# Three more filler products, and the weights' low part split before the second pair of inputs, in the opening of a GRU, attention and FFN kernel

## What is computed

```python
def cell(h, x):
    gi = x @ W_ih + b_ih
    gh = h @ W_hh + b_hh
    i_r, i_z, i_n = jnp.split(gi, 3, axis=-1)
    h_r, h_z, h_n = jnp.split(gh, 3, axis=-1)
    r = jax.nn.sigmoid(i_r + h_r)
    z = jax.nn.sigmoid(i_z + h_z)
    n = jnp.tanh(i_n + r * h_n)
    h_new = (1.0 - z) * n + z * h
    return (h_new, h_new)
```

## Time and profile before

| what | us |
|---|---|
| median of three runs | 617.98 |
| lowest and highest | 616.83, 618.19 |
| the profiled execution's own time | 617.67 |
| its span | 615.9 |

### The profile page before, as it was taken

The page is one execution under the profiler, slowest core; times in us unless marked ns, Lnnn a source line. Parts: engine busy times, 40 slices in busy tenths (PEclk is TensorE's granted clock), DMA queues, the critical chain, the costliest instruction groups (busy, mean ns, idle before and its releaser), DMA issues.

```text
span 615.9 us, 14207 instructions
## 1 busy us (share of the span) xinstructions
PE 581.6 (94%) x4918; PEld 526.5 (85%) x4918; DVE 516.6 (84%) x1544; ACT 404.8 (66%) x982; POOL 256.2 (42%) x401
## 2 busy tenths in 40 slices
PE   8999999999999879998888999999999999999997
PEld 7999999999999878887776888888888887888875
DVE  2776777776767768888988999999999999999996
ACT  3545454544445456575446888888888888888885
POOL 0333323232332353420144555555565565565550
PEclk9999999999999999998999999999999999999999
DMA  8400000000000000500000000000000000000001
GB/s 267 169 2 1 2 1 2 1 1 2 1 1 1 19 1 1 186 1 1 2 0 2 10 11 18 19 10 18 19 18 11 19 18 10 19 20 10 18 19 34
DMA packets 12517, 14.87 MB, mean 24 GB/s; under 512 B 1632, under 2 KB 10144, under 8 KB 12448
## 3 DMA queue, kind: packets, MB, share of 16 engines
q1 hardware_dynamic: 12448, 13.97, 6.8%
HBM read 9.78 MB, written 4.19 MB: 23 GB/s over the span
## 4 chain that ended last, share of the span: by engine, by line
PE 69%; DVE 13%; ACT 12%; issue 3%; SPq 1%; DMA 1%; POOL 0%; DVEq 0%; ACTq 0%
PE PS L451 22%; PE PS L313 16%; PE PS L336 12%; ACT q_s L756 4%; PE PS L503 3%; PE PS L524 3%; ACT k_s L737 2%; PE PS L487 2%; PE PS L429 2%; PE PS L389 2%; PE PS L372 2%; ACT big L669 2%; DVE PS L1052 1%; DVE big L934 1%; ACT PS L740 1%
## 5 line engine op out<-in xcount | busy, mean ns | idle before, releaser
L451 PE MATMUL PS<-k_s,h_s 128*128 128x128 f32 x1024 | 160.7, 285 | 4.6 <-DVE PS L1032 1.9
L451 PEld LDWEIGHTS PS<-k_s,h_s 128*128 128x128 f32 x1024 | 131.7, 191 | 22.0 <-DVE PS L1040 10.0
L313 PE MATMUL PS<-part 128*128 128x256 f32 x900 | 115.6, 286 | 0.0
L313 PEld LDWEIGHTS PS<-part 128*128 128x128 f32 x900 | 109.8, 191 | 0.0
L737 ACT ACTIVATE k_s<-h_s 128x128 f32<-128x128 f32 x256 | 69.1, 306 | 50.5 <-DVE h_s L1137 29.1
L336 PE MATMUL PS<-big,wrk 128*128 128x128 f32 x744 | 88.4, 275 | 2.2 <-DVE big L891 2.2
L336 PEld LDWEIGHTS PS<-big,wrk 128*128 128x128 f32 x744 | 85.8, 192 | 2.8 <-DVE big L891 2.8
L1200 POOL COPY h_s<-big 128x256 f32<-128x256 f32 x32 | 21.5, 671 | 131.2 <-DVE big L891 131.2
L451 PE MATMUL PS<-h_s 128*128 128x128 f32 x384 | 74.2, 275 | 0.0
L451 PEld LDWEIGHTS PS<-h_s 128*128 128x128 f32 x384 | 58.3, 192 | 0.0
L634 ACT ACTIVATE big<-big 128x256 f32<-128x256 f32 x32 | 13.3, 417 | 63.8 <-DVE big L873 63.8
(11 more groups left out here) (184 smaller groups left out, 1277.8 us busy)
## 6 DMA issues: line engine op xcount, KB each, us to landing
out<-q_s SPq DMA_DIRECT2D x32, 128.0 KB, 1.7
x_s<-in_xT SPq DMA_DIRECT2D x14, 256.0 KB, 6.1
k_s<-in_wgT SPq DMA_DIRECT2D x1, 832.0 KB, 5.2
k_s<-in_wuT SPq DMA_DIRECT2D x1, 832.0 KB, 7.1
k_s<-in_wih SPq DMA_DIRECT2D x3, 256.0 KB, 4.0
wrk<-in_whh SPq DMA_DIRECT2D x3, 256.0 KB, 4.9
h_s<-in_wdT SPq DMA_DIRECT2D x1, 768.0 KB, 7.6
x_s<-in_xT SPq DMA_DIRECT2D x4, 128.0 KB, 3.7
```

Source lines behind the costliest of these rows:

```text
L313: r = pe.matmul(p, y, x, start=i == 0, stop=i == len(passes) - 1)
L451: return pe.matmul(PS[:, m, 0:128], w, x, start=False, stop=True, skip_group_check=True)
```

## The change

Three edits, all in what is issued before the loop over the steps. SyncE issues the load of the last third of `W_hh` (gate z) behind the second pair of x, not ahead of it. TensorE makes eleven products of ones in place of eight. VectorE makes `wih_lo` right after `wih_hi`, ahead of the two splits of x. No instruction is removed, the computed result is the same, and every line of the kernel behind L256 has a number that is one higher.

```diff
-            for i in (0, 2, 1):
+            for i in (0, 2):
                 sp.dma_start(wcut(whh_s, i), wcut(kp(whh), i)).then_inc(ld_whh[i], 16)
             for k in range(2):
                 sp.dma_start(x0[:, k, 2:4], xv[:, k, 2:4, :]).then_inc(ld_x0[1], 16)
+            sp.dma_start(wcut(whh_s, 1), wcut(kp(whh), 1)).then_inc(ld_whh[1], 16)
...
-            keep_warm(0, 8)
+            keep_warm(0, 11)
...
             ve.tensor_copy(raw(wih_hi), wih_s).then_inc(s_wih, 1)
+            ve.wait_ge(s_wih, 1)
+            ve.tensor_tensor(raw(wih_lo), wih_s, wih_hi, ALU.subtract).then_inc(s_wih, 1)
             ve.wait_ge(ld_x0[1], 32)
             ve.tensor_copy(raw(x_hi[1]), x_s[:, :, 256:512]).then_inc(s_x1, 1)
             ve.wait_ge(s_x1, 1)
             ve.tensor_tensor(raw(x_lo[1]), x_s[:, :, 256:512], x_hi[1], ALU.subtract).then_inc(s_x1, 1)
-            ve.wait_ge(s_wih, 1)
-            ve.tensor_tensor(raw(wih_lo), wih_s, wih_hi, ALU.subtract).then_inc(s_wih, 1)
```

## The result

| what | changed | before |
|---|---|---|
| median of four runs, us | 614.06 | 617.40 |
| lowest and highest | 613.36, 614.19 | 616.18, 618.19 |
| the profiled execution's own time | 613.96 | 617.67 |
| its span | 612.0 | 615.9 |

The ratio is 0.9945, with a 95% interval of 0.9925 to 0.9966. Both have to be explained.

A forecast was written before the change was run, and what follows sets the result against it. The opening was taken as bound by VectorE, TensorE right behind, and the rest by TensorE's work. With the clock rising at 6.4 us the gate addition comes 1.9 us earlier: 617.98 - 1.9 = 616.1 us, range 615.3 to 617.8.

The forecast's parts named there:

- What bounds the opening: Before the first gate addition: VectorE is late by 0.5 us, with TensorE right behind it.
- The moved subtraction is free: The weights' low part, 1.75 us, fits VectorE's 3.0 us wait for x; by itself it gains 0.5 us.
- The load of x: Second pair of x lands 0.5 to 0.7 us earlier; z's weights land at 11.8 at the latest, costing nothing.
- the rival without it: Opening: x lands no sooner, at 11.52 us, VectorE free at 12.7; gain 1.6 us, time 616.4; chance 0.09.
- The rise of the clock, C: Time when TensorE's clock rises in the opening, taken as 6.4 us; gate addition then at 12.4 instead of 14.29.
- not before 4.8: Lower bound on the clock's rise in the opening, since fillers up to there are all slow in the trace.
- My sum for the time of r's products: Opening: input products end at C / 2 + 8.04, r's products begin 0.03 later, at 11.27 us.
- The rest is the same length: After the opening everything shifts as a whole, so the opening's 1.9 us gain lasts to the end.
- The size: Whole kernel: 1.9 us gained, from 617.98 to 616.1 us.
- The clock rises no sooner: Opening: the clock rise stays near 9.4 us, gain 0.4, time 617.6; chance 0.24 for little or no sooner.
- it does nothing: Whole kernel: the runs' spread covers the gain or a later wait pays it back; 618.0 us, chance 0.07.
- later: slower: Opening: the clock rises later, or not during the input products, which gives 620.9 us; chance 0.06.

The follow-up runs named there:

- turn_after: The changed kernel with GpSimd's last three attention subtractions made to wait for VectorE's multiplication of the same block: 612.89 us, ratio 0.9927.
- after: The changed kernel itself, with all three edits against the kernel before, as first measured and profiled: 614.06 us, ratio 0.9945.
- turn_after_2: The same kernel as turn_after, run once more on another chip: 613.36 us, ratio 0.9932.
- after_again: The changed kernel with nothing further altered, run twelve more times: 615.62 us, ratio 0.9969.
- warm_sum: The changed kernel with four further fillers directly ahead of each of three weight summations, on another chip: 614.83 us, ratio 0.9966.
- turn_split_only: The kernel before with only the weights' low part moved, plus GpSimd's late subtractions behind VectorE's multiplications, on another chip: 613.63 us, ratio 0.9941.
- turn_fill11_only: The kernel before with eleven fillers, nothing moved in the opening, plus GpSimd's late subtractions behind VectorE's multiplications: 614.80 us, ratio 0.9957.
- turn_fill8: The changed kernel with eight fillers instead of eleven, plus GpSimd's late subtractions behind VectorE's multiplications: 614.52 us, ratio 0.9949.

## Why the prediction was wrong in its range and right in its mechanism

- **What bounds the opening: right.** VectorE was last by 0.5 us with TensorE right behind. Where TensorE was last, as in turn_after, the gate addition started 1.16 us after r's first product; 1.1 had been taken. The fillers without the split's move give nothing (617.14, and 614.80 against 614.89), and with a late clock the moves without the fillers give 0.2 to 0.5 us (third steps at 23.59 and 23.36 against 23.83).
- **The moved subtraction is free: right.** It ran at 9.07 to 10.83 us, 0.5 us later than forecast since the biases landed later, in VectorE's wait for x. The cover is thinner than thought: in this profile VectorE went on without idling, so it, not the landing, was last there.
- **The load of x: right, with a scatter larger than the move.** The second pair of x landed at 10.3 to 11.7 us in the eight profiles with the new order and at 10.8 to 12.2 in the six with the old one, on average at 10.8 and 11.5. So 0.75 us were won where 0.5 to 0.7 were forecast. The gate addition started at 11.8 to 12.8 us in the five profiles of the whole change, right behind VectorE in three (after, turn_after_2, after_again) and behind TensorE in two (turn_after, warm_sum). In time the order was forecast to be worth 0.3 us (the rival without it gains 1.6 instead of 1.9), and it was 0.3, not clear of the noise. Its cost was taken too lightly: z's weights landed as late as 12.45 us (after_again), not at 11.8 at the latest, 0.4 us before TensorE came to them.
- **The rise of the clock, C: mis-sized.** I took 6.4 us; it was 4.8, and in eight of the nine profiles with more fillers it was earlier than I took it. With the early landing of x that made 2.49 us in the profile instead of 1.9. The bound "not before 4.8" was no bound: it came from one trace, and the clock rose at 4.3 us in after_again and turn_split_only and at 4.6 in turn_after. My sum for the time of r's products was right: turn_fill11_only, with r's products at 11.67, gives C = 2 x (11.67 - 8.07) = 7.2, and the input products, 5.99 us against 5.35 at the full pace, bear that out. The reason for C was too simple, since a gap of 0.7 us neither forbids an early rise nor undoes it. The Trainium skill ("TensorE: Matmul & The Clock Gate", section "What you observe") was right that the point differs from run to run, but by its half microsecond to either side one would not expect 9.4 us in one profile and 4.3 in another of eight fillers.
- **"The rest is the same length": the step that failed.** This is what put the time outside the range. It is the same work, but its time isn't the same: 589.0 without the tie, 590.7 with it, 592.3 with the clock's fall behind it. The rows of before held the sign. L925's longest was 2.83 us against a median of 0.73, and PEclk of the page shows an 8 in one slice. The forecast took 1.9 us off 617.98, which is the level of the runs in which the clock fell (their median on record is 617.97, and the profiled run is one of them), and all four runs of the result were of those in which it didn't. From the other level, 616.58, the same 1.9 us lead to 614.7. I read the chain only up to 60 us, and took the spread of 1.4 us between three runs for a property of the measurement. A range for the median of a few runs has to hold this spread on the new kernel's side as well.
- **The size.** 1.9 us were forecast. The pair without the tie gives 2.0, the twelve further runs 1.5 with an interval of 1.0 to 2.8 (ratio 0.9954 to 0.9984). The measured 3.3 us are 2.0 to 2.5 from the opening and about 1 from four runs in which the clock did not fall, which their granted clock of 1.000 shows. That part was luck: it fell in six of the twelve later runs of the same kernel.
- **The rivals.** "The clock rises no sooner" and "it does nothing" did not occur with the whole change, and "later: slower" never came near.

What stays open: why eight fillers gave an early clock in one of six runs of turn_fill8 and in some four of six of turn_split_only, on another chip; what makes VectorE or GpSimd win a tie; and what decides whether the clock falls after a wait of 1.9 us.

## What to carry to other kernels

Two engines that become ready within half a microsecond of each other hide each other's gain, so cost the edits together. Here the fillers alone gave 0.1 us; the split alone gave about 1.1 us by the ratios (0.9941 against 0.9959), because the clock rose early without the fillers in four of its six runs. Before pricing a change of 2 us, look for instructions whose longest duration is several times their median, in the whole span, since they tell what the rest will do to the comparison, and compare runs whose granted clocks are alike: 617.40 to 614.06 looks like 3.3 us, and like with like it was 1.7 to 2.3. Here putting GpSimd's last three subtractions behind VectorE's multiplications was worth 2.4 us in the kernel before, more than the change itself, and with the change it is the best version measured: 612.89 us, 0.9927 of before.

## What the runs showed of the hardware

- Two elementwise instructions of VectorE (two SBUF inputs, 128x512 fp32) and GpSimd (128x1024) that start within 0.1 us of each other don't share evenly: the winner takes its usual time, and the loser ends about 0.5 us after it where VectorE loses. VectorE took 2.83 to 2.91 us instead of 0.69 (once in each of six profiles), GpSimd 2.91 to 2.92 instead of 2.36 (in two). Which wins changed between runs and blocks.
- After an idle stretch of TensorE of 1.9 to 2.1 us the clock stayed up in one profile and fell to its 1.2 GHz level for some 3.5 us in four (granted clock 0.50). After 1.0 us it did not fall in warm_sum's profile, nor after the 1.5 us at the third mean in any.
- In five profiles with the same eight fillers the clock rose at 9.2 to 9.5 us three times and before 5.5 us twice. With eleven or fourteen it rose at 4.3 to 7.2 us in nine.
- One and the same load of x (2 x 128 KB, the same place in the queue) landed at 10.3 to 11.7 us in eight profiles.
